# Head weights of a transformer tower on one core: the grams as moving side of the products, VectorE's multiply-and-sum, and a changed order of loads

## The reference, cut to what matters

```python
h = tokenizer(x)                          # q k^T * gate, v, Wo, PReLU
mn = layernorm(h) * gamma + beta
q, k = (mn @ Wq), (mn @ Wk)               # 8 heads of 32
v, g = (mn @ Wv), sigmoid(mn @ Wg + bg)
att = softmax_t(einsum('slhc,tlhc->sth', q, k) / sqrt(32) / sqrt(4096))
h = h + (einsum('sth,tlhc->slhc', att, v) * g) @ Wo + bo
h = h + ffn(layernorm(h))                 # top half of the tokens by router weight
```

## Time and profile before

| | us |
|---|---|
| median of 3 runs | 2031.94 (2031.43 to 2033.35) |
| profiled execution, its own time | 2031.88 |
| its span, first to last instruction | 2030.2 |
| TensorE busy | 1968.6 (97%) |
| VectorE, ScalarE, GpSimd busy | 1221.4, 691.1, 455.6 |

### The profile page before, as it was taken

One profiled execution on the slowest core, in us unless ns is written; L12 is line 12 of the kernel. 1 busy time (PEld: TensorE's weight loads), 2 busy tenths in 40 slices (PEclk: granted clock), 3 DMA queues, 4 the chain that ended last, 5 costly groups with the idle time before them and its releaser, 6 DMA issues.

```text
span 2030.2 us, 27454 instructions
## 1 busy us (share of the span) xinstructions
PE 1968.6 (97%) x9494; PEld 1629.8 (80%) x9494; DVE 1221.4 (60%) x2229; ACT 691.1 (34%) x1119; POOL 455.6 (22%) x582
## 2 busy tenths in 40 slices
PE   8999999999999999999999999999999999939998
PEld 7788888888888888888888888888887888828897
DVE  5646565665656566766565656565565548867553
ACT  5422222222222225522222222222223537625554
POOL 4202020202102022420120202021120347623442
PEclk9999999999999999999999999999999999959999
DMA  4232433333242433233424333333424659721110
GB/s 156 85 108 83 152 113 125 115 124 126 91 166 96 143 113 127 83 104 125 155 72 160 123 116 113 124 107 122 145 84 155 213 183 313 271 67 57 43 43 32
DMA packets 87843, 250.14 MB, mean 123 GB/s; under 512 B 11697, under 2 KB 32177, under 8 KB 87729
## 3 DMA queue, kind: packets, MB, share of 16 engines
q1 hardware_dynamic: 83296, 240.26, 35.1%
q0 software_dynamic: 3072, 8.44, 1.3%
q10 hardware_dynamic: 1360, 0.01, 0.0%
HBM read 194.05 MB, written 54.62 MB: 122 GB/s over the span
## 4 chain that ended last, share of the span: by engine, by line
PE 91%; DVE 3%; issue 2%; ACT 2%; DMA 1%; POOL 0%; SPq 0%; DVEq 0%; ACTq 0%; POOLq 0%
PE bank L676 35%; PE bank L691 35%; PE bank L1637 5%; PE bank L834 4%; PE bank L1658 4%; PE bank L1206 2%; PE bank L646 1%; PE bank L722 1%; PE bank L620 1%; PE bank L630 1%; PE bank L723 1%; DVE kt L490 1%; PE bank L661 1%; PE bank L860 1%; DVE vf L501 0%
## 5 line engine op out<-in xcount | busy, mean ns | idle before, releaser
L691 PE MATMUL bank<-x_hi,kt 128*128 128x512 f32 x2048 | 723.9, 395 | 1.5 <-DVE work L528 1.4
L528 DVE SCALAR_TENSOR_TENSOR work<-bank,d_col,gate 128x512 f32<-128x512 f32 x512 | 383.9, 750 | 553.4 <-PE bank L691 544.3
L405 ACT ACTIVATE p_hi<-work 128x512 fp32r<-128x512 f32 x512 | 324.0, 633 | 1065.4 <-PE bank L676 1020.5
L691 PEld LDWEIGHTS bank<-x_hi,kt 128*128 128x128 f32 x2048 | 384.4, 188 | 90.4 <-DVE work L528 2.5
L676 PE MATMUL bank<-p_hi,v_hi 128*128 128x512 f32 x1024 | 407.0, 397 | 0.3 <-ACT yT L367 0.2
L676 PE MATMUL bank<-p_hi,v_lo 128*128 128x512 f32 x1024 | 404.1, 395 | 0.0
L676 PE MATMUL bank<-p_lo,v_hi 128*128 128x512 f32 x1024 | 403.4, 394 | 0.0
L691 PE MATMUL bank<-x_lo,kt 128*128 128x512 f32 x1024 | 400.9, 391 | 0.0
L516 DVE TENSOR_TENSOR p_lo<-work,p_hi 128x512 fp32r<-128x512 f32 x512 | 367.6, 718 | 29.3 <-ACT p_hi L405 29.2
L579 POOL TENSOR_SCALAR spread<-mv 128x4 f32<-128x4 f32 x16 | 3.9, 243 | 1124.5 <-DVE mv L459 1124.5
L676 PEld LDWEIGHTS bank<-p_hi,v_hi 128*128 128x128 f32 x1024 | 192.2, 188 | 50.6 <-DVE p_lo L516 5.3
(11 more groups left out here) (235 smaller groups left out, 2325.0 us busy)
## 6 DMA issues: line engine op xcount, KB each, us to landing
gate<-in_gateT SPq DMA_DIRECT2D x256, 512.0 KB, 3.6
work<-in_xT SPq DMA_DIRECT2D x32, 512.0 KB, 5.1
scratch_rows<-rows SPq DMA_DIRECT2D x16, 518.0 KB, 3.8
scratch_h<-work SPq DMA_DIRECT2D x16, 512.0 KB, 3.0
scratch_mn<-mn_sb SPq DMA_DIRECT2D x16, 512.0 KB, 6.7
scratch_mT_hi<-mT_hi SPq DMA_DIRECT2D x16, 512.0 KB, 2.7
scratch_mT_lo<-mT_lo SPq DMA_DIRECT2D x16, 512.0 KB, 4.0
gate<-scratch_mn SPq DMA_DIRECT2D x16, 512.0 KB, 4.3
```

Of the source, the lines that this page charges most:

```text
L405: nc.scalar.activation(p_hi[:, i % 2, :], p32[:, i % RP, :], ACT.Copy).then_inc(hi_done, 1)
L528: nc.vector.scalar_tensor_tensor(p32[:, i % RP, :], S[i % 2][:, :], d_col[:, i:i + 1], gate[:, g % RG, j, :], ALU.add, ALU.mult).then_inc( ...
L691: mm = pe.matmul(S[i % 2][:, :], w, x, start=n == 1, stop=n == 3 * KD)
```

## The change

In `head_weights` each 128-column block of wq and wk is the stationary side and the gram the moving side, so that the product has the heads' columns on the partitions. The other factor must then be turned too: TensorE transposes wq and wk (eight 128 x 128 transposes into banks 3 and 2), ScalarE copies them to `qT` and `kT`. The products come in eight sets; the first four cover G(0,0) and G(0,1) side by side in 512 columns, the last four G(1,1) in 256. VectorE multiplies each half of a set by the turned weight and sums along the row in one operation (`tensor_tensor_reduce`, twelve of them), which writes a column of `cols`. The matmuls with ones and the copy of their sums go; the sum by head is two matmuls that accumulate. On SyncE, `step(0, 0)` (m tiles of chunk 1, h tiles of chunk 0) stands in front of the MLP's loads and waits for `g_done` alone; the MLP's loads wait for the eighth set.

```diff
-def head_weights(pr, W2, heads_in, grams, banks, M):
+def head_weights(pr, W2, heads_in, grams, banks, M, ident):
...
+    lefts = ((wk, wqT, 0), (wq, wkT, 1))
+    rows = [(w, m, g0, n) for g0, n in ((0, 2 * D), (2, D)) for w in range(2) for m in range(KD)]
+    def products_of(i):
+        w, m, g0, _ = rows[i]
+        if g0 == 2:
+            return ((slice(0, D), w, 3 * KD + m),)
+        cross = (1 if w == 1 else 2) * KD + m
+        return ((slice(0, D), w, m), (slice(D, 2 * D), 0, cross))
+    before_set = [sum(len(products_of(e)) for e in range(i)) for i in range(SETS + 1)]
...
         pe.wait_ge(kept, 4)
-        for i, (g0, c0, w) in enumerate(((0, 0, wk), (0, 0, wq), (0, D, wq), (0, D, wk), (2, 0, wk), (2, 0, wq))):
-            if i >= 3:
-                pe.wait_ge(prod_ok, i - 2)
+        pe.wait_ge(ld, 16 * 7)
+        for w, bank in ((wq, banks[3]), (wk, banks[2])):
             for m in range(KD):
                 for k in range(KD):
-                    mm = pe.matmul(TP[i % 3][:, m, :], grams[:, g0 + k, c0 + m * P:c0 + (m + 1) * P], w[:, k, :],
-                                   start=m == 0 and k == 0, stop=k == KD - 1, skip_group_check=True)
+                    t = pe.transpose(bank[:, m * D + k * P:m * D + (k + 1) * P], w[:, k, m * P:(m + 1) * P], ident[:, :])
+            t.then_inc(turned, 1)
+        for i, (w, m, g0, n) in enumerate(rows):
+            if i == 2:
+                pe.wait_ge(turned_kept, 2)
+            if i >= 3:
+                pe.wait_ge(cols_ok, before_set[i - 2])
+            for k in range(KD):
+                mm = pe.matmul(banks[i % 3][:, 0:n], lefts[w][0][:, k, m * P:(m + 1) * P], grams[:, g0 + k, 0:n],
+                               start=k == 0, stop=k == KD - 1)
             mm.then_inc(tp, 1)
         pe.wait_ge(made, 2 + P // head)
-        for i, of in enumerate((0, 0, 1, 2, 3, 3)):
-            pe.wait_ge(prod_ok, i + 1)
...
-                    mm = pe.matmul(colp[:, at:at + 2], prod[:, i, m, j * P:(j + 1) * P], heads_in["ones"][:, :],
...
-        pe.wait_ge(cols_sb, 1)
-        pe.matmul(attp, heads_in["same_head"][:, :], cols[:, :], start=True, stop=True).then_inc(att_ok, 1)
+        pe.wait_ge(cols_ok, before_set[SETS])
+        pe.matmul(attp, heads_in["same_head"][:, :], cols[:, 0, :], start=True, stop=False)
+        pe.matmul(attp, heads_in["same_head"][:, :], cols[:, 1, :], start=False, stop=True).then_inc(att_ok, 1)
         values_and_gates(pr, pe, W2, M, 0, 0, 1)
...
-        dve.wait_ge(ld, 16 * 7)
-        for i, w in enumerate((wq, wk, wk, wq, wq, wk)):
+        dve.wait_ge(turned_kept, 2)
+        dve.wait_ge(made, 2 + P // head)
+        for i, (w, m, _, _) in enumerate(rows):
             dve.wait_ge(tp, i + 1)
-            nc.vector.tensor_tensor(prod[:, i], TP[i % 3][:, :, :], w[:, :, :], ALU.mult).then_inc(prod_ok, 1)
-        dve.wait_ge(col_ok, 1)
-        nc.vector.tensor_copy(cols[:, :], colp).then_inc(cols_sb, 1)
+            for e, (few, part, to) in enumerate(products_of(i)):
+                nc.vector.tensor_tensor_reduce(out=prod[:, before_set[i] + e, :], in0=banks[i % 3][:, few],
+                                               in1=lefts[w][1][:, m, :], scale=1.0, scalar=0.0, op0=ALU.mult, op1=ALU.add,
+                                               accum_out=cols[:, part, to:to + 1]).then_inc(cols_ok, 1)
...
     @block.scalar
     def _(act):
+        for i, (t, bank) in enumerate(((wqT, banks[3]), (wkT, banks[2]))):
+            act.wait_ge(turned, i + 1)
+            nc.scalar.activation(t[:, :, :], bank[:, :].rearrange("p (m n) -> p m n", m=KD), ACT.Copy).then_inc(turned_kept, 1)
         act.wait_ge(step, 4)
...
-            sp.wait_ge(pr.sem("hw_tp"), 6)
+            sp.wait_ge(pr.sem("g_done"), NC)
+            step(0, 0)
+            sp.wait_ge(pr.sem("hw_tp"), 8)
             sp.dma_start(mlp_raw["w1"], ins["ffn_w1"].rearrange("(k p) n -> p k n", p=P)).then_inc(raw_ld, 16)
...
-            chunks(step)
+            for c in range(1, NC + 2):
+                step(c, c % 2)
```

More of the change, by code:

```diff
@@ L771, in _ @@
         nc.gpsimd.memset(heads_in["same_head"][:, :], 0.0).then_inc(made, 1)
-        nc.gpsimd.memset(heads_in["ones"][:, :], 1.0).then_inc(made, 1)
+        nc.gpsimd.memset(heads_in["cols"][:, :, :], 0.0).then_inc(made, 1)
         pool.wait_ge(made, 2)
@@ L842, in head_weights @@
     scale = head ** -0.5 * pr.T ** -0.5
-    wq, wk, prod, cols, att = (heads_in[n] for n in ("q", "k", "prod", "cols", "att"))
+    wq, wk, wqT, wkT, prod, cols, att = (heads_in[n] for n in ("q", "k", "qT", "kT", "prod", "cols", "att"))
     top, shifted, expd, total, inv = (heads_in[n] for n in ("top", "shifted", "expd", "total", "inv"))
[L845 to L848, removed]
+    attp = banks[3][:, 64:72]
+    ld, made, kept, tp, cols_ok, att_ok, step, exp_ok = (pr.sem(n) for n in (
+        "hw_ld", "hw_made", "hw_kept", "hw_tp", "hw_cols", "hw_att", "hw_step", "hw_exp"))
+    turned, turned_kept = pr.sem("hw_turned"), pr.sem("hw_turned_kept")
     block = pr.block
+    lefts = ((wk, wqT, 0), (wq, wkT, 1))
+    rows = [(w, m, g0, n) for g0, n in ((0, 2 * D), (2, D)) for w in range(2) for m in range(KD)]
+    SETS = len(rows)
+    def products_of(i):
[5 more added lines that the diff above has]
+    before_set = [sum(len(products_of(e)) for e in range(i)) for i in range(SETS + 1)]
     @block.tensor
@@ L853, in _ @@
         pe.wait_ge(kept, 4)
-        for i, (g0, c0, w) in enumerate(((0, 0, wk), (0, 0, wq), (0, D, wq), (0, D, wk), (2, 0, wk), (2, 0, wq))):
-            if i >= 3:
-                pe.wait_ge(prod_ok, i - 2)
+        pe.wait_ge(ld, 16 * 7)
+        for w, bank in ((wq, banks[3]), (wk, banks[2])):
             for m in range(KD):
                 for k in range(KD):
-                    mm = pe.matmul(TP[i % 3][:, m, :], grams[:, g0 + k, c0 + m * P:c0 + (m + 1) * P], w[:, k, :],
-                                   start=m == 0 and k == 0, stop=k == KD - 1, skip_group_check=True)
+                    t = pe.transpose(bank[:, m * D + k * P:m * D + (k + 1) * P], w[:, k, m * P:(m + 1) * P], ident[:, :])
[8 more added lines that the diff above has]
+                               start=k == 0, stop=k == KD - 1)
             mm.then_inc(tp, 1)
         pe.wait_ge(made, 2 + P // head)
-        for i, of in enumerate((0, 0, 1, 2, 3, 3)):
-            pe.wait_ge(prod_ok, i + 1)
-            for j in range(KD):
-                for m in range(KD):
-                    at = 4 * of + 2 * j
-                    mm = pe.matmul(colp[:, at:at + 2], prod[:, i, m, j * P:(j + 1) * P], heads_in["ones"][:, :],
-                                   start=i == 0 and j == 0 and m == 0, stop=m == KD - 1 and i not in (0, 4),
-                                   skip_group_check=True)
-        mm.then_inc(col_ok, 1)
-        pe.wait_ge(cols_sb, 1)
-        pe.matmul(attp, heads_in["same_head"][:, :], cols[:, :], start=True, stop=True).then_inc(att_ok, 1)
+        pe.wait_ge(cols_ok, before_set[SETS])
+        pe.matmul(attp, heads_in["same_head"][:, :], cols[:, 0, :], start=True, stop=False)
+        pe.matmul(attp, heads_in["same_head"][:, :], cols[:, 1, :], start=False, stop=True).then_inc(att_ok, 1)
         values_and_gates(pr, pe, W2, M, 0, 0, 1)
@@ L882, in _ @@
             nc.vector.tensor_copy(grams[:, i, 0:n], banks[i][:, 0:n]).then_inc(kept, 1)
-        dve.wait_ge(ld, 16 * 7)
-        for i, w in enumerate((wq, wk, wk, wq, wq, wk)):
+        dve.wait_ge(turned_kept, 2)
+        dve.wait_ge(made, 2 + P // head)
+        for i, (w, m, _, _) in enumerate(rows):
             dve.wait_ge(tp, i + 1)
-            nc.vector.tensor_tensor(prod[:, i], TP[i % 3][:, :, :], w[:, :, :], ALU.mult).then_inc(prod_ok, 1)
-        dve.wait_ge(col_ok, 1)
-        nc.vector.tensor_copy(cols[:, :], colp).then_inc(cols_sb, 1)
+            for e, (few, part, to) in enumerate(products_of(i)):
+                nc.vector.tensor_tensor_reduce(out=prod[:, before_set[i] + e, :], in0=banks[i % 3][:, few],
+                                               in1=lefts[w][1][:, m, :], scale=1.0, scalar=0.0, op0=ALU.mult, op1=ALU.add,
+                                               accum_out=cols[:, part, to:to + 1]).then_inc(cols_ok, 1)
         dve.wait_ge(att_ok, 1)
-        nc.vector.tensor_copy(att[:, :, :, :], banks[3][:, 64:80:2].rearrange("p (s t j) -> p s t j", s=2, t=2)).then_inc(step, 1)
+        nc.vector.tensor_copy(att[:, :, :, :], banks[3][:, 64:72].rearrange("p (s t j) -> p s t j", s=2, t=2)).then_inc(step, 1)
         dve.wait_ge(step, 1)
@@ L1745, in build @@
                 heads_in = {n: sb(nc, heads_phase, f"hw_{n}", shape) for n, shape in (
-                    [("same_head", [P, P]), ("ones", [P, 2])] + [(x, [P, KD, width]) for x in ("v", "g", "k", "q")] +
-                    [("o", [P, KD, width + 2]), ("o_wr", [P, KD, width]), ("prod", [P, 6, KD, width]), ("cols", [P, 16]),
```

(4 more changed lines are left out.)

## The result

| | before | changed |
|---|---|---|
| median of 8 runs | 2031.86 (2031.23 to 2034.53) | 2027.2 (2026.74 to 2027.94) |
| ratio to before, 95% interval | | 0.9975 (0.9966 to 0.9984) |
| profiled execution, its own time | 2031.88 | 2027.0 |
| its span | 2030.2 | 2025.3 |

The kernel is faster by 4.66 us. The forecast was 2026.5 and rival A 2028.2; the median lies between, and the profiles fit that: of four executions of the changed kernel that were profiled, two went as the forecast said and two as A said.

The account below looks back on a forecast made before the run. Up to 1655.95 a TensorE sequence and a transfer were taken to end nearly together. The head sum 4.06 us earlier and full clock, less a 2.4 us og_lo wait, start L1206 5.45 earlier: 2031.9 - 5.45 = 2026.5 us, range 2025.6 to 2029.1.

Parts of the forecast that it names:

- The forecast: Whole kernel: 2026.5 us, L1206 starting 5.45 us earlier and the gain kept; chance 0.52.
- rival A: Gap before L1206: clock falls to half for some 3.3 us, costing 1.7, so 2028.2 us; chance 0.35.
- What bounds the kernel: Up to 1655.95 a TensorE sequence and a transfer end nearly together; the m-tile wait itself is 0.65 us.
- Transposes: Head part, before the products: eight 128x128 fp32 transposes add 0.87 us on the path, upper bound 1.3 more.
- Products: Gram products in 512 and 256 columns: 10.37 us, unchanged; upper bound 0.55 more.
- VectorE's product and sum from PSUM: Replaces 48 matmuls: 0.42 + 0.08 us each as L472; only the last on the path, 0.50 plus 0.05 semaphores.
- Head sum: After the last VectorE product: starts at 1642.18, 4.06 us earlier.
- Clock behind it: Behind the head sum: granted clock 1.00, so the second values and gates cost 5.59 us.
- m tiles: Chunk 1's loads issued at g_done (1624.8) land by some 1637, 11 us early, with no wait for them.
- The next bound: Before L1206: TensorE waits 2.4 us for the third og_lo and starts at 1656.2 against 1661.65.
- The clock in that gap: In the new 2.4 us gap before L1206: full clock in the forecast, half clock costing 1.7 us in rival A.
- The nearer row shows no fall: Argument against rival A: a gap of 1.99 us left the clock at 1.00; after 3.09 it was 0.50.

Follow-up runs that it names:

- e1: Changed kernel with the loads back in their old order (MLP weights first): 2033.13 us, ratio 1.0002 to the kernel before.
- e2: Kernel before with only the loads moved: 2031.35 us, ratio 0.9994 to the kernel before.
- e5: e4b with wq and wk also laid out turned in memory, no transposes or ScalarE copies: 2025.36 us, ratio 0.9964 to the kernel before.
- e4b: Changed kernel with the two-value softmax as a sigmoid, its table loaded early, second set of runs: 2024.02 us, ratio 0.9962 to the kernel before.
- after_again: The changed kernel run again without alteration: 2027.55 us, ratio 0.9977 to the kernel before.
- e7: Changed kernel with every VectorE product-and-sum issued twice, the second into spare tiles: 2028.71 us in one execution, 2033.54 for the kernel before.

## Why the prediction was right

- **What bounds the kernel** (two things that end nearly together at 1655.95): shown by e1 and e2, each part alone within 0.1% of no change.
- **Transposes**: 0.87 predicted, 0.87 on the chain, and 0.88 by e5 against e4b. The Trainium skill's 275 ns for a bf16 transpose (TensorE: Matmul & The Clock Gate, Part 4: PE-mode transpose), taken as a cost, would be 2.2 us for eight, an estimate that these fp32 rows do not bear out.
- **Products**: 10.37 predicted, 10.34 measured. An fp32 instruction of 512 columns costs twice one of 256 (eight in 3.43 us, 1633.91 to 1637.34, and in 1.73, to 1639.07); the upper bound (0.55 more) did not come.
- **VectorE's product and sum from PSUM**: 0.42 and 0.08, as L472's from SBUF, and the next one starts 0.35 after the one before, which is the lowest bound as a pace. On the path the last one cost 0.61 from the last product to the head sum (1640.97 to 1641.58); 0.57 was predicted.
- **Head sum**: predicted at 1642.18, 17.40 after the stage's begin; measured 17.41.
- **Clock behind it**: 1.00, so the two values and gates behind the head sum take 11.29 (11.18 by twice 5.59).
- **m tiles**: issued at 1624.2 to 1625.5 and landed 4.2 to 7.0 us later, so by about 1632.5 (1637 was said); no wait for them. The row of these loads:

```profile
DMA to landing us min/median/max: 4.2/5.5/7.0
```

- **The next bound**: third `og_lo`, wait of 2.4 predicted, 2.11 measured, since TensorE is ready 0.25 later than summed (29.29 after the stage's begin, 29.04 predicted: the head sum and the two values and gates cost a little more). L1227 starts 31.40 after the begin of the stage (31.42 predicted; 36.87 before), so 5.47 sooner against 5.45. e4b shows the cause, as above. No further wait in the mix: 101.36 to its last chunk before and after.
- **The clock in that gap**, the point at which forecast and A part: both happen. The stage was forecast at 34.44 (39.89 less 5.45) and is 34.52; A's is 36.14 and 35.99 and 35.96 were measured. The step that was left too sharp is this one: one kernel was given one outcome, where each execution draws its own. A mix of the two fits the median (4.66 less in the first set of runs, 4.67 in the second), which lies between A's 3.7 and the forecast's 5.4; the medians carry other draws of the clock too, so that is argued.
- **Why the forecast was put before A**: each of the two rows was one draw. In the twelve profiles of the table the gap of 1.99 to 2.01 us ahead of L722, the same code in all, is followed by half clock in ten, and the gap of 3.09 in seven. "The nearer row shows no fall" was the luck of one execution, and 0.52 against 0.35 had no support in it. That the number came within 0.7 us is in part luck: the two outcomes came about equally often.

Not part of any step: where the stage begins. after_again has the better stage and the longer own time of the first two profiles of the changed kernel, because its stage begins 2.62 later.

## What to carry to other kernels

Where a chain shows two things that end within a microsecond of each other, price both parts of a change together: each alone is worth next to nothing, and one alone may cost. When work is taken off the engine that paces a kernel, follow the dependent chain on the other engines to its end, since its length is the next bound, and a gap that it leaves on TensorE may or may not cost the clock: what one profile shows behind such a gap is one draw, not a bound. When an effect is a thousandth of the time, compare a stretch of the chain between two points where the instructions are the same in both kernels, over several profiles, and not one total.

## What the runs showed that was not expected

- The same gap of 2.1 us gave a granted clock of 0.50 for 3.4 us (1655.4 to 1658.8) in one execution and 1.00 in another of the same kernel: two of four. The cost was 1.45 to 1.47 us on L1227 (4.57 and 4.59 against 3.12).
- Code that no kernel here changes varied more than some of the changes: the tokenizer's end by 3.0 us (1623.81 to 1626.79), and the stretch before the choice of tokens by 1.7 us. The clock accounts for most of it, at three places, by the twelve profiles of the table. First, at the program's start, the eight matmuls of L169 take 1.97 to 1.98 us in seven and 3.45 to 3.76 in five, and what follows them is 2.0 to 2.4 later in these five; that this is half clock is read from the pace alone. Second, the fall of the clock behind the gap of 1.99 to 2.01 us ahead of L722 costs 1.5; it came in ten, and stayed away only in the kernel before and e5. So the tokenizer ends at 1623.8 to 1624.5 (early start, fall), at 1624.78 and 1625.61 (late start, no fall) or at 1626.4 to 1626.8 (late start, fall). Third, behind the gap of 3.09 the clock fell in seven, and the stretch to the choice takes 43.36 to 44.61 there; it stayed at 1.00 in five, with 42.95 to 42.98 (43.28 in e7; why is open). Rows of the changed kernel's first profile (timeline, then windows with columns as above), and behind them L169 in after_again:

```profile
10.86 1.98 PE L169 MATMUL bank<-wo,wvT 128*128 128x256 f32 x8
1575.73 0.49 PE L722 MATMUL bank<-kt 128*128 128x512 f32 x1 [2.00 <-DVE kt L554]
1773.06 0.36 PE L1227 MATMUL bank<-wo_hi,og_hi 128*128 128x258 f32 x1 [3.09 <-DVE w_raw L1088]
1578.00:1580.00 2.00, 2.00 (x7) 1.61 (x7) 2.00 (x2) 0.00 (x0) 1.95 (x1) 0.50 0.97 360
1774.60:1774.80 0.20, 0.20 (x4) 0.20 (x3) 0.20 (x1) 0.00 (x0) 0.05 (x1) 1.00 0.00 0
```

```profile
11.44 3.76 PE L169 MATMUL bank<-wo,wvT 128*128 128x256 f32 x8
```
